# First attention with float32r projections: the masked scores of a group made by ACT and GpSimd, not by VectorE

## What is computed

```python
def feature_map(t, K):                       # per head: 64 -> 128 features
    f = einsum('hdf,bhld->bhlf', K, t)
    feats = concatenate([softmax(f), softmax(-f)], -1)
    return maximum(feats, 1e-12)
q, k, v = heads(x @ Wq), heads(x @ Wk), heads(x @ Wv)      # x normalised
qf, kf = feature_map(q, Kq), feature_map(k, Kk)
kv = cumsum(kf[:, :, :, None, :] * v[..., None], axis=2)   # causal
o = einsum('bhlf,bhldf->bhld', qf, kv)
z = einsum('bhlf,bhlf->bhl', qf, cumsum(kf, axis=2)) + 1e-12
x = x + (o / z[..., None]) @ Wo
```

## Time and profile before

| what | value |
|---|---|
| median of 3 runs | 1231.16 us (1226.87 to 1235.7) |
| the profiled execution | 1229.25 us, span 1227.0 us from first to last instruction |
| mean granted TensorE clock | 0.982 of full speed |
| busy over the whole span: PE, DVE, ACT, POOL | 1117.3, 962.1, 611.1, 377.3 us |
| the first attention's tile work | from 51 us (first scores) to about 541 us |

### The profile page before, as it was taken

One profiled execution on the slowest core, in us unless ns is written; L12 is line 12 of the kernel. 1 busy time (PEld: TensorE's weight loads), 2 busy tenths in 40 slices (PEclk: granted clock), 3 DMA queues, 4 the chain that ended last, 5 costly groups with the idle time before them and its releaser, 6 DMA issues. The chain is left out here.

```text
span 1227.0 us, 30062 instructions
## 1 busy us (share of the span) xinstructions
PE 1117.3 (91%) x11860; PEld 719.6 (59%) x11861; DVE 962.1 (78%) x1769; ACT 611.1 (50%) x1166; POOL 377.3 (31%) x355
## 2 busy tenths in 40 slices
PE   6698898899899999879999999999999957999996
PEld 5577777777788878643443344334444334666765
DVE  6889978987888788888788677877889556777757
ACT  4233343334333433227777677776788822444443
POOL 4432245222522222113201320222110414656651
PEclk9899999999999999999999999999999988999998
DMA  7100001000400000524720570065050144221225
GB/s 240 41 8 1 2 28 53 2 1 1 80 2 2 1 1 2 81 59 81 152 34 8 114 146 2 9 127 108 2 211 3 53 80 145 65 64 60 63 62 205
DMA packets 60045, 73.65 MB, mean 60 GB/s; under 512 B 14404, under 2 KB 51140, under 8 KB 59188
## 3 DMA queue, kind: packets, MB, share of 16 engines
q1 hardware_dynamic: 56132, 61.56, 21.0%
q0 software_dynamic: 3792, 10.36, 2.7%
HBM read 52.86 MB, written 18.78 MB: 58 GB/s over the span
## 5 line engine op out<-in xcount | busy, mean ns | idle before, releaser
L1791 DVE TENSOR_REDUCE neg_max<-pS 128x1 f32<-128x1024 f32 x238 | 284.9, 1220 | 56.2 <-PE pS L1574 56.0
L1706 ACT ACTIVATE pt<-pR 128x512 f32<-128x512 f32 x512 | 286.5, 600 | 80.1 <-PE pR L1597 75.3
L1597 PE MATMUL pR<-qs,ks 100*32 100x512 bf16 x2048 | 191.2, 383 | 3.1 <-ACT pt L1706 1.6
L1574 PE MATMUL pS<-ks,qs 100*32 100x512 bf16 x1904 | 145.9, 381 | 5.1 <-issue 1.9
L1611 PE MATMUL b_pO<-pt,b_v 128*32 128x512 f32 x1024 | 135.9, 605 | 2.9 <-ACT pt L1706 2.3
L1597 PEld LDWEIGHTS pR<-qs,ks 100*32 100x32 bf16 x2048 | 56.2, 96 | 95.3 <-issue 25.6
L324 POOL TENSOR_TENSOR kf<-kf,fsum 128x2048 f32<-128x2048 f32 (+1 forms) x17 | 58.2, 3422 | 163.8 <-DVE fsum L933 163.8
L324 POOL TENSOR_TENSOR qs<-qs,fsum 128x2048 f32<-128x2048 f32 (+1 forms) x17 | 58.5, 3446 | 142.7 <-DVE fsum L933 142.7
L1453 POOL COPY qs<-max_rows 3x512 bf16<-3x512 bf16 x60 | 36.6, 610 | 209.3 <-ACT max_rows L1699 206.3
L745 ACT COPY qfT<-pT 128x512 f32<-128x512 f32 x64 | 37.3, 582 | 122.7 <-PE pT L466 122.7
L1574 PEld LDWEIGHTS pS<-ks,qs 100*32 100x32 bf16 x1904 | 51.4, 97 | 74.3 <-issue 35.7
(11 more groups left out here) (376 smaller groups left out, 2270.8 us busy)
## 6 DMA issues: line engine op xcount, KB each, us to landing
qs<-q_scr SPq DMA_DIRECT2D x24, 256.0 KB
ks<-k_scr SPq DMA_DIRECT2D x7, 768.0 KB
k_scr<-f SPq DMA_DIRECT2D x18, 256.0 KB, 2.8
ks<-in_L_ffn_w_dram SPq DMA_DIRECT2D x2, 2048.0 KB, 11.1
ks<-in_L_ffn_w_dram SPq DMA_DIRECT2D x4, 1024.0 KB, 8.5
ks<-y_rows SPq DMA_DIRECT2D x16, 256.0 KB, 5.1
ks<-k_scr SPq DMA_DIRECT2D x6, 512.0 KB
cx<-in_ctx_dram SPq DMA_DIRECT2D x3, 768.0 KB, 12.3
```

What stands on the lines that cost most here:

```text
L1574: ins = pe.matmul(pS1[q:q + XV, slot, 512 * half:512 * half + 512], qs[0:KR, bass.ds(par, 1), h, P * t + q:P * t + q + XV].rearrange("r a ...
L1597: ins = pe.matmul(ring[bank][q:q + XV, :], ks[0:KR, bass.ds(par, 1), h, P * j + q:P * j + q + XV].rearrange("r a n -> r (a n)"), qs[0:KR, ...
L1706: nc.scalar.activation(pt[:, j % 2, i, :], ring[bank], ACT.Exp).then_inc(exp_done, 1)
L1791: nc.vector.tensor_reduce(neg_max[:, hg % 2, u // G, u % G:u % G + 1], pS1[:, u % 2, :], AX_X, ALU.max, negate=True).then_inc(max_done, 1)
```

## The change

A mask is made in two steps. ACT copies the scores of a group from PSUM to `am` (`scores_copy`, new semaphore `a_copied`), and GpSimd multiplies `am` in place with `causal` (`mask`, now in its sequence, still counted by `a_masked`). The bank `pA` is free for the next scores after ACT's copy; the outputs wait for GpSimd's product. VectorE has no masks any more. On ACT a v copy moves ahead of a preparation. On GpSimd the constants (and the turning of two weights) move into a function that is called behind mask(0, 1).

```diff
@@ GpSimd
+                def mask(t, g):
+                    wait(pool, a_copied, 4 * t + g + 1)
+                    pool.wait_ge(s_k, 8)
+                    nc.gpsimd.tensor_tensor(am[:, g % 2], am[:, g % 2], causal[:, :].unsqueeze(1).broadcast_to([P, G, P]),
+                                            ALU.mult).then_inc(a_masked, 1)
+
+                mask(0, 0)
                 scale(0, 1, 1)
...
-                        if not (last and c == TB - 1):
-                            scale(1, TB * b + c + 1, (c + 1) % 2)
+                        t, par = TB * b + c, c % 2
+                        has1, has2 = not (last and c == TB - 1), not (last and c >= TB - 2)
+                        mask(t, 1)
+                        if (b, c) == (0, 0):
+                            constants()
+                        mask(t, 2)
+                        if has1:
+                            scale(1, t + 1, 1 - par)
+                        mask(t, 3)
                         if (b, c) == (0, TB - 1):
                             split_k(0)
                             split_k(1)
-                        if not (last and c >= TB - 2):
-                            scale(0, TB * b + c + 2, c % 2)
+                        if has1:
+                            mask(t + 1, 0)
+                        if has2:
+                            scale(0, t + 2, par)
@@ TensorE, chunk_scores
-                    wait(pe, a_masked, 4 * t + g)
+                    wait(pe, a_copied, 4 * t + g)
@@ ACT
+                def scores_copy(t, g):
+                    wait(act, a_done, 4 * t + g + 1)
+                    wait(act, o_done, 4 * t + g - 1)
+                    nc.scalar.copy(am[:, g % 2], pA[:, :, :]).then_inc(a_copied, 1)
+
...
                         f_copies(t, 1)
+                        scores_copy(t, 1)
                         prepare(prep, 0)
                         prepare(prep, 1)
                         f_copies(t, 2)
                         if has1:
                             exponentials(1, t + 1, 0, 1 - par)
+                        scores_copy(t, 2)
                         prepare(prep, 2)
                         prepare(prep, 3)
                         f_copies(t, 3)
                         if has1:
                             exponentials(1, t + 1, 1, 1 - par)
+                            v_copy(t + 1, 0, 1 - par)
+                        scores_copy(t, 3)
                         prepare(prep, 4)
-                        if has1:
-                            v_copy(t + 1, 0, 1 - par)
@@ VectorE
-                def mask(t, g):
-                    wait(dve, a_done, 4 * t + g + 1)
-                    wait(dve, o_done, 4 * t + g - 1)
-                    nc.vector.tensor_tensor(am[:, g % 2], pA[:, :, :],
-                                            causal[:, :].unsqueeze(1).broadcast_to([P, G, P]),
-                                            ALU.mult).then_inc(a_masked, 1)
...
-                            if g < G - 1:
-                                mask(t, g + 1)
```

More of the change, by code:

```diff
@@ L169, in linear_attention @@
         fT_ready = [sem("kT"), sem("qT")]
-        a_done, a_masked = sem("a_done"), sem("a_masked")
+        a_done, a_copied, a_masked = sem("a_done"), sem("a_copied"), sem("a_masked")
         d_done, s_upd = sem("d_done"), sem("state")
@@ L330, in _ @@
                         scale(m, 0, 0, hs, half_of)
-                scale(0, 1, 1)
[L333 to L347, removed]
+                def mask(t, g):
[3 more added lines that the diff above has]
+                                            ALU.mult).then_inc(a_masked, 1)
@@ new lines, in _, with constants @@
+                mask(0, 0)
+                scale(0, 1, 1)
+                def constants():
+                    pool.memset(last_row[:, :], 0.0).then_inc(s_k, 1)
+                    pool.wait_ge(s_k, 9)
+                    pool.affine_select(out=last_row[:, :], in_=last_row[:, :], compare_op=ALU.not_equal, fill=1.0,
+                                       base=-(KR - 1), pattern=[[0, 1]], channel_multiplier=1).then_inc(s_k, 1)
+                    pool.memset(q_aug[:, :], 0.0).then_inc(s_k, 1)
+                    pool.memset(zero[:, :], 0.0).then_inc(s_k, 1)
+                    pool.memset(max_parts[:, :, :, :], 0.0).then_inc(s_k, 1)
+                    pool.wait_ge(s_k, 12)
+                    pool.wait_ge(s_c, 48)
+                    for s in range(2):
+                        nc.gpsimd.tensor_copy(ck[:, s, :].rearrange("p (d h) -> p d h", h=XH),
+                                              ck_raw[:, s, :].rearrange("p (h d) -> p d h", h=XH)).then_inc(c_turned, 1)
+                    for k in range(KD):
+                        nc.gpsimd.tensor_copy(cq[:, k, :].rearrange("p (d h) -> p d h", h=XH),
+                                              cq_raw[:, k, :].rearrange("p (h d) -> p d h", h=XH)).then_inc(c_turned, 1)
@@ L589, in turn_maxima @@
                     pe.wait_ge(prep_copied, PREPARED + 1)
-                    pe.wait_ge(a_masked, 4 * T)
+                    pe.wait_ge(a_copied, 4 * T)
                     turned = pA[:, :, :].rearrange("p h n -> p (h n)")
@@ L799, in _ @@
                 f_copies(0, 0)
+                scores_copy(0, 0)
                 exponentials(0, 1, 1, 1)
@@ L846, in batch @@
                             exponentials(0, t + 2, 1, par)
+                        if has1:
+                            scores_copy(t + 1, 0)
                 batch(0, False)
@@ L1070, in _ @@
                 shift(0, 1, 1, 1, own)
-                dve.wait_ge(s_k, 6)
-                mask(0, 0)
                 denominators(0, 1, 1, own)
@@ L1129, in batch @@
                         wait(dve, x1_done, t + 1)
-                        if has1:
-                            mask(t + 1, 0)
                         if last and c == TB - 2:
```

## The result

The changed kernel takes 1295.57 us (1292.51 to 1297.34), the kernel before beside it 1231.01: 1.0521 times as long [1.0478, 1.0563]. Slower, as predicted, but by 64 us and not by 30; the range ended at 1276. The profiled execution took 1292.51 us (span 1290.8) at a mean granted clock of 0.943, against 0.982 before.

A forecast was written before the change was run, and what follows sets the result against it. TensorE was taken to bound the first attention, VectorE next. New waits 26.1 + 10.2 + 1.0 + 17.4, clock 4.0, less gains 28.6, gave +30.1 us on 1229.25: 1259 us, range 1238 to 1276.

The forecast's parts named there:

- the mechanism of the waits: First attention: mask 3 queues on GpSimd behind the next tile's late scale of q, later masks behind splits; TensorE waits.
- I count no clock for the waits of 2.9: TensorE's waits at mask 3, first attention: the clock stays full, as in the steady part before; cost 0.
- 4.0 us for the clock: Slow clock after the two waits of 8.7 us behind the splits: 2 us each, ends 0 and 9.
- TensorE stands at mask 3 anyway: Tiles 4 and 8, 7 us after the splits' wait: mask 3's wait limits the clock's loss to 2 us each.
- the new waits: TensorE waiting for GpSimd's masks: 26.1 in nine tiles, 10.2 in batch 0, 1.0 in tiles 7 and 11, 17.4 at splits.
- The chain: Tile 6, q's exponential to mask 3: 1.09 to sum, 2.32 to reciprocal, 0.44 to scale, 3.62 scale, 1.17 mask; wait 2.9.
- the gains: TensorE waits for VectorE that vanish: masks 8.8, state 13.8, `x_rest` 3.1, tile 15 2.9; sum 28.6 us.
- a predicted 3.1: Waits for `x_rest`, the next transposed input's low part: only the two long ones, 2.2 and 2.7, fall to 0.92.
- The gains without the queue: Rival: mask 3 reaches TensorE in time, only the splits cost; 1218 us, faster; chance 0.10.
- half the wait: Rival: latencies in mask 3's chain overlap more, 37.3 us of waits become 18; 1238 us, no change; chance 0.12.
- The shared port: Rival: GpSimd's masks slow VectorE's SBUF operations, up to 1.0 us in 14 tiles; 1273 us; chance 0.12.
- The copies on ACT: First attention: ACT's 64 score copies are free, as ACT idles over half the stage; 0.59 us each if uncovered.

The follow-up runs named there:

- The experiment that puts one call ahead of another: Changed kernel with mask 3 ahead of the scale of q on GpSimd instead of behind it: 1229.75 us, 0.9981 of the kernel before.
- spare matmuls: Changed kernel plus TensorE transposes of the identity, 24 ahead of waits for mask 3, 60 ahead of the two at the splits: 1262.54 us, ratio 1.0259.
- the version with both moved: Changed kernel with mask 3 ahead of the scale of q, and split operations behind that scale in the next batch's first tile: 1212.70 us, ratio 0.9864.
- Moving the splits alone: Changed kernel with only split_k 2, 3 and split_q 0, 1 behind the scale of q in the next batch's first tile: 1275.57 us, ratio 1.0363.
- the kernel without the product: Changed kernel without GpSimd's multiplication with the causal matrix; outputs wait for ACT's copies: 1200.19 us, ratio 0.9740.
- the fastest versions: Changed kernel with mask 3 ahead of the scale and splits moved, 1212.70 us; with L385's power and ACT's first score copy also later, 1208.04 us.
- three kernels: Changed kernel, 1295.57 us, and it with GpSimd's scale of q cut around mask 3 into 12 + 4 heads, 1276.10, or 8 + 8, 1256.51.
- with 8 heads first and with 12: Changed kernel with GpSimd's scale of q in two parts, mask 3 between: 8 heads first 1256.51 us (1.0202), 12 first 1276.10 us (1.0366).

## Why the prediction was right and wrong

**Right: the bound, the sign and the mechanism of the waits.** TensorE waits for mask 3 in twelve tiles, and for a mask behind the splits in two. The experiment that puts one call ahead of another takes 66 us off the changed kernel, so the place in GpSimd's queue is the cause, and not the product itself.

**Wrong: the step "I count no clock for the waits of 2.9".** This is the term that failed: 4.0 us for the clock, with ends of 0 and 9, where TensorE's matmuls took 27.1 longer and spare matmuls gave 27.4 back. The step drew two things from the rows of before that they don't bear. A full clock while TensorE has no matmul says nothing of what comes after it; in tile 6 too, the clock is full during the wait and falls at its end. And waits of up to 2.67 without a fall were taken to cover waits of 2.9, though they are those of one execution: the mean clock of the 20 others of this kernel on record lay between 0.975 and 0.986, that of the profiled one at 0.982. A wait of 2.73 for `x_rest` in the version with both moved was followed by 0.50, and waits of 1.5 went both ways. Behind the wait stands the k projection, and nothing hides its longer matmuls. Where the prediction did count clock, behind the splits, 4.0 was too much but its reason held: "TensorE stands at mask 3 anyway". Moving the splits alone gave back 0.6 us of busy time, and the waits at mask 3 of tiles 4 and 8 grew from 2.85 and 3.27 to 3.93 and 3.94.

**Undersized: the new waits, 54.7 predicted, 62.2 measured.** The chain was right to 0.01 in each link, but the mask takes 1.29 us and not 1.17, TensorE starts 0.15 behind its end, and in the nine tiles the mean wait is 3.27 and not 2.9: 3.3 us in all. Batch 0 gave 11.3 for 10.2, tiles 7 and 11 together 1.7 for 1.0, the splits 17.8 for 17.4. The power ahead of mask 1, which stood in the code and not in the sum, cost 2.0. These make the 7.5.

**Too high: the gains, 28.6 predicted, some 24 measured.** The masks' 8.8 went whole. The state's went from 13.8 to 3.1 and not to 0: a residue of 2.0 lies in batch 0. `x_rest` fell by 3.0 for a predicted 3.1, but for another reason than the one given, so the number was luck. Where TensorE isn't late it stays at 13.9 to 14.1, so its two long waits do not hang on the masks; in the changed kernel TensorE came later to them. Had nothing been added, the gain would have been the 23.5 of the kernel without the product. In tile 15 TensorE's waits for the maxima, two rows before and one after, fell by 1.9 for a predicted 2.9:

```profile
PE pP L582 <- DVE neg_max L1025: 3.6, 4, 1.2
...
PE pDW L582 <- DVE neg_max L1025: 0.4, 1, 0.4
...
PE pP L600 <- DVE neg_max L1046: 2.2, 3, 1.2
```

So the gains in the changed kernel come to 8.8 + 10.7 + 3.0 + 1.9 = 24.4, and the sum closes: 62.2 + 27.1 - 24.4 = 64.9, against 64.5 in the stage.

**The rivals.** "The gains without the queue" and "half the wait" fall with the chain of tile 6; the order that the first of them needs is the one that the fastest versions have. "The shared port" is there, but with little in the time: VectorE's waits for it delay nothing in tile 6's chain to mask 3, whose links kept their length, and the product in a fitting order costs 6 to 8 us of the stage, waits for masks and all. The prediction's reading of the earlier trace rows, 0.82 for each of four scalings, is a mean that misleads; the first took 2.31, until the scale beside it was done, and the other three 0.40 (shortest, median and longest in ns):

```profile
L1018 DVE TENSOR_SCALAR ks<-xr,x_mv,x_rstd x4: 402/402/2309, 230.8 to 233.6; 128x256 f32<-128x256 f32 x4
```

GPSIMD Engine Reference of the Trainium skill (Key points) has GpSimd share its SBUF interfaces with VectorE; the clamp's 1.22 us with GpSimd at rest and 1.39 beside a mask agree with it. Its figure for an operation on two tensors (3.1), 4497 ns for 2048 elements, would give 1.12 us as an estimate for a quarter; the trace has 3.62 for the scale of 2048, 1.05 for its part of 512 and 1.29 for the mask of 512, so a quarter of the long one (0.91) is not the price of a short one either.

**The copies on ACT** were rightly free: no row of TensorE's waits in the changed kernel's stage names them.

## What to carry to other kernels

When work moves to an engine that was idle, read where it enters that engine's queue: behind a long operation that itself comes late, a wait appears that no busy share shows, and moving one call may be worth more than the move of the work. Price a new wait on TensorE at its length and at the matmuls behind it at half speed, here some 2 us for each of the waits of about 3, and let the range reach down to no such loss rather than take one execution whose waits did no harm for a rule. What spare matmuls in the waits give back is a direct measure of that second part.

## What the runs showed of the hardware

- The clock falls behind short waits too. Of the 36 waits at mask 3 in three kernels it came to 0.50 at 16 of 16 of 2.67 to 4.39 us, at 7 of 10 of 2.0 to 2.5 and at 3 of 10 of 1.2 to 1.8, from 1.7 us before the end of the wait to 2.4 behind it. In tile 6 of the changed kernel it was at 0.50 from 293.4 to 300.2 us. In the kernel before a wait of 2.67 had no fall.
- Matmuls whose result nobody reads keep it up: 408 of them took the stage's clock from 0.90 to 0.99 and the program from 1295.57 to 1262.54 us.
- On GpSimd the scale costs 3.62 us for 2048 elements per partition, 2.76 for 1536, 1.91 for 1024 and 1.05 for 512; the mask, 512 with another broadcast, costs 1.29. Cutting a scale in two cost 0.2 us. The parts, with 8 heads first and with 12:

```profile
L384 POOL TENSOR_TENSOR qs<-qs,fsum 128x1024 f32<-128x1024 f32 x30 | 57.2, 1905 | 80.0 <-DVE fsum L971 80.0
...
L384 POOL TENSOR_TENSOR qs<-qs,fsum 128x1536 f32<-128x1536 f32 x15 | 41.4, 2763 | 79.4 <-DVE fsum L971 79.4
L384 POOL TENSOR_TENSOR qs<-qs,fsum 128x512 f32<-128x512 f32 x15 | 15.7, 1046 | 0.0
```

- VectorE's clamp of k and scaling of x, between SBUF tiles, wait for a GpSimd operation that is already running: a clamp of 1.22 us took 1.39 with 0.31 us of a mask left, 4.26 beside copies and a mask. Reductions and subtractions from PSUM kept their time.
